# Cross-attention with a routed expert layer: the last 65 context rows laid out anew

## The reference

```
q = layernorm(x) @ Wq.T ; k = ctx @ Wk.T ; v = ctx @ Wv.T
attn = einsum('bhnc,bhlc->bhnl', q * 256 ** -0.5, k)
attn = softmax(attn, axis=2)
attn = attn / sum(attn, axis=-1, keepdims=True)
x = x + tanh(g_xattn) * (einsum('bhnl,bhlc->bhnc', attn, v) @ Wo.T)
x = x + tanh(g_ffn) * experts(layernorm(x))
```

## Time and profile before

| what | value |
|---|---|
| runs of the kernel before | 1812.7, 1813.04, 1815.76 us; median 1813.04 |
| profiled execution | 1814.16 us, span 1812.4 us |
| setup and first projections | to about 30 us of the span |
| attention, 8 batches | about 30 to 1245 us |
| turn to the experts, and the experts | 1245 us to the end |
| period of a middle batch | 152.6 us |
| mean granted clock | 0.991 |

### The profile page before, as it was taken

One profiled execution on the slowest core, in us unless ns is written; L12 is line 12 of the kernel. 1 busy time (PEld: TensorE's weight loads), 2 busy tenths in 40 slices (PEclk: granted clock), 3 DMA queues, 4 the chain that ended last, 5 costly groups with the idle time before them and its releaser, 6 DMA issues.

```text
span 1812.4 us, 31594 instructions
## 1 busy us (share of the span) xinstructions
PE 1683.1 (93%) x9980; PEld 900.1 (50%) x9980; DVE 1419.2 (78%) x2293; ACT 1283.9 (71%) x3640; POOL 542.7 (30%) x825
## 2 busy tenths in 40 slices
PE   8989999999999989999999998887799999999997
PEld 5223233333333323333333332214799999999997
DVE  7979999999999999999999999997444444444442
ACT  5989999999999999999999999995111111111111
POOL 3331251352244225235223422213222222222222
PEclk9999999999999999999999999999899999999999
DMA  8547215613711731461272163419222222222221
GB/s 233 129 112 189 63 51 148 162 40 96 196 53 52 176 108 47 133 181 40 75 194 60 58 162 83 148 54 299 86 35 38 36 37 35 38 35 38 35 36 28
DMA packets 128245, 172.87 MB, mean 95 GB/s; under 512 B 14496, under 2 KB 105760, under 8 KB 128128
## 3 DMA queue, kind: packets, MB, share of 16 engines
q1 hardware_dynamic: 113152, 150.51, 30.3%
q0 software_dynamic: 14144, 20.44, 6.5%
q10 hardware_dynamic: 832, 0.53, 0.1%
HBM read 117.96 MB, written 53.47 MB: 95 GB/s over the span
## 4 chain that ended last, share of the span: by engine, by line
PE 36%; ACT 29%; DVE 20%; issue 7%; POOL 3%; DMA 3%; SPq 1%; POOLq 0%; DVEq 0%; ACTq 0%
ACT w_all L899 27%; DVE negmax L1080 14%; PE scores L1474 13%; PE scores L1487 13%; PE scores L716 3%; PE acc L729 3%; POOL routed_rows L1273 1%; DVE resid L975 1%; ACT w_all L857 1%; DMA out<-row_t,gate_token 1%; PE spare L579 1%; PE spare L573 1%; PE spare L1464 1%; DVE rz L1066 1%; SPq L389 1%
## 5 line engine op out<-in xcount | busy, mean ns | idle before, releaser
L899 ACT ACTIVATE w_all<-scores,negmax 128x512 f32<-128x512 f32 (+1 forms) x1664 | 1127.8, 751 | 24.8 <-DVE negmax L1080 19.3
L1080 DVE TENSOR_REDUCE negmax<-scores 128x2 f32<-128x1024 f32 (+1 forms) x832 | 1002.2, 1216 | 65.6 <-PE scores L716 59.2
L716 PE MATMUL scores<-q_stack,w_all 128*128 128x512 bf16 (+1 forms) x1664 | 501.9, 383 | 50.0 <-ACT w_all L899 48.3
L899 ACT ACTIVATION_READ_ACCUMULATOR w_all<-scores,negmax 128x1 f32 (+1 forms) x1664 | 449.3, 270 | 0.0
L729 PE MATMUL acc<-w_all,vz 128*32 128x512 f32 (+1 forms) x3328 | 443.7, 605 | 3.0 <-POOL vz L1296 2.8
L1515 ACT ACTIVATE projections<-scores 128x512 f32<-128x512 f32 x142 | 84.9, 598 | 449.0 <-PE scores L1474 449.0
L716 PEld LDWEIGHTS scores<-q_stack,w_all 128*128 128x128 bf16 (+1 forms) x1664 | 115.7, 99 | 524.9 <-ACT w_all L899 395.5
L1296 POOL TENSOR_TENSOR vz<-w_all,rz 128x68 f32<-128x68 f32 (+1 forms) x416 | 124.7, 300 | 789.3 <-DVE rz L1066 763.7
L1474 PEld LDWEIGHTS scores<-row_t,q_stack 128*128 128x128 f32 x2272 | 265.9, 193 | 7.6 <-issue 2.8
L1474 PE MATMUL scores<-row_t,q_stack 128*128 128x128 f32 x2272 | 267.5, 276 | 2.0 <-DVE row_t L1542 1.8
L1487 PE MATMUL scores<-room,projections 128*128 128x256 f32 x1136 | 256.8, 379 | 0.0
(11 more groups left out here) (208 smaller groups left out, 1027.8 us busy)
## 6 DMA issues: line engine op xcount, KB each, us to landing
w_all<-k_parts SPq DMA_DIRECT2D x248, 200.1 KB, 3.5
w_all<-in_w SPq DMA_DIRECT2D x16, 1024.0 KB, 10.8
q_stack<-q_parts SPq DMA_DIRECT2D x248, 64.0 KB, 3.4
k_parts<-parts SPq DMA_DIRECT2D x42, 300.0 KB, 2.9
w_all<-in_ctx_t SPq DMA_DIRECT2D x7, 1601.0 KB, 7.3
parts<-routed SPq DMA_DIRECT2D x71, 129.0 KB, 2.1
q_parts<-parts SPq DMA_DIRECT2D x14, 384.0 KB, 3.2
routed<-pad_row SPq DMA_DIRECT2D x8, 645.0 KB, 9.5
```

What stands on the lines that cost most here:

```text
L716: mm = pe.matmul(scores[0:r, 2 * (u % SLOTS) + j % 2, :], k_stacks[g][:, j, lt * P:lt * P + r], q_stack[:, g, j, :], start=True, stop=True)
L899: e = act.activation(probs[0:r, s % RING, j, :], scores[0:r, 2 * (u % SLOTS) + j % 2, :], ACT.Exp, bias=negmax[0:r, u % 4, j % 2:j % 2 + 1 ...
L1080: dve.tensor_reduce(negmax[0:r, u % 4, :], scores[0:r, 2 * (u % SLOTS):2 * (u % SLOTS) + 2, :], AX.X, ALU.max, negate=True).then_inc(negma ...
```

## The change

The 65 rows of the last tile are split: 64 rows (`REST`) and the row 1600 (`LONE`).

- **Two heads in a tile.** The last step of a group (`lt == LT`, now 12) has one unit instead of two. Four matmuls of 64 columns of weights put heads 0 and 1 into one bank, one at partitions 0 to 63 and the other at 64 to 127, and heads 2 and 3 into the other bank. One reduction and two exponentials do for the four heads. The values of the tile stand twice, in both halves of the partitions, and are multiplied by 0 or 1 (`own_rows`) so that each head finds only its own half; `weigh` uses one bank of exponentials for two heads.
- **The lone row.** Row 1600 of all 16 heads stands in one tile. The context gets columns of zeros around row 1600 (`LK` = 1635 columns, `lone_apart` on the input), and matmuls of 32 columns of weights, shifted by the group, put head j of group g at partition 32 j + g and zeros elsewhere, adding up over the groups. In batches 1 to 7 this is one extra unit of 16 matmuls, one reduction of 512 and one exponential at the last step of group 0 (step 12); in batch 0 it is done for two groups at a time, after groups 0 and 2 (`lone_groups`). Its values (row 1600 on all partitions, masked by head) are scaled once by GpSimd (`lone_vz`), and every `weigh` of a last tile gets four more matmuls with them.
- **Units are counted through** over all batches (`units_by`), and each waits for `u - SLOTS + 1`. A batch has 101 units (102 in the first).
- **The last value piece** (tiles 12 and 13, the doubled 64 rows and the lone row) is done in two halves like the others, one step later in the table (48 for 47; in the first batch 7 for 6), and is taken by VectorE with the mask instead of by ScalarE; two fills behind it move on by one.
- VectorE writes the masks at the start with some 30 small memsets.

```diff
-LT = (L + P - 1) // P
+LT = L // P
+LAST_TILE = LT * P
+REST = L - 1 - LAST_TILE
+LONE = LAST_TILE + REST
+LONE_AT = LONE + H // 4 - 1
+LK = LONE_AT + TAIL_ROWS
+VT = LT + 2
+GROUP_STEPS = LT + 1
...
-    47: ("next", "v", 6), 48: ("cur", "attn_turn", 0), 49: ("cur", "o_turn", 2),
+    48: ("next", "v", 6), 49: ("cur", "attn_turn", 0), 50: ("cur", "o_turn", 2),
...
+def lone_groups(b, g):
+    if b == 0:
+        return range(g, g + 2) if g % 2 == 0 else range(0)
+    return range(G) if g == 0 else range(0)
+
+def units_of(b, s):
+    g, lt = s // GROUP_STEPS, s % GROUP_STEPS
+    return 2 if lt < LT or len(lone_groups(b, g)) else 1
...
         def project_v(bank, i, halves):
+            for lt in (2 * i + h for h in halves):
+                cols = slice((lt % 2) * D, (lt % 2 + 1) * D)
                 for k in range(KC):
+                    if lt == LT:
+                        for twice in range(2):
+                            mm = pe.matmul(bank[REST * twice:REST * (twice + 1), cols], ctx_sb[:, k, LAST_TILE:LAST_TILE + REST],
+                                           wv_sb[:, k, :], start=(k == 0), stop=(k == KC - 1))
+                    else:
+                        rows = ctx_sb[:, k, lt * P:(lt + 1) * P] if lt < LT else ctx_sb[:, k, LONE_AT:LONE_AT + 1].to_broadcast([P, P])
+                        mm = pe.matmul(bank[:, cols], rows, wv_sb[:, k, :], start=(k == 0), stop=(k == KC - 1))
...
         def unit_scores(b, s, p):
+            if p >= units_of(b, s):
+                return
...
-            wait(pe, exp_done, b * UNITS + (u - SLOTS + 1 if u >= SLOTS else (-1, 0, -2)[u]))
+            if lt == LT and p == 1:
+                for of in lone_groups(b, g):
+                    stack_here(b, of)
+            wait(pe, exp_done, u - SLOTS + 1)
...
+            elif p == 0:
+                for j in range(GH):
+                    mm = pe.matmul(scores[REST * (j % 2):REST * (j % 2 + 1), bank + j // 2, :],
+                                   k_stacks[g][:, j, LAST_TILE:LAST_TILE + REST], q_stack[:, g, j, :], start=True, stop=True)
+            else:
+                groups = lone_groups(b, g)
+                for of in groups:
+                    for j in range(GH):
+                        mm = pe.matmul(scores[32 * j:32 * j + TAIL_ROWS, bank, :],
+                                       k_stacks[of][:, j, LONE_AT - of:LONE_AT - of + TAIL_ROWS], q_stack[:, of, j, :],
+                                       start=(of == groups[0]), stop=(of == groups[-1]))
...
         def weigh(b, s):
...
+                mm = pe.matmul(acc[32 * j:32 * j + 32, :], vz[:, s % RING, j, :],
+                               probs[:, s % RING, j if lt < LT else j // 2, :], start=(lt == 0), stop=False)
+            if lt == LT:
+                pe.wait_ge(lone_vz_ready, lone_units(b, g))
+                for j in range(GH):
+                    mm = pe.matmul(acc[32 * j:32 * j + DH + 1, :], lone_vz[:, g * GH + j, :], lone_probs[:, :],
+                                   start=False, stop=True)
...
+            elif name in ("v", "own_v"):
+                dve.tensor_tensor(v_ones[(b + 1 if name == "v" else b) % 2][:, LT:VT, :, 0:DH],
+                                  spare[:, :].rearrange("p (t h c) -> p t h c", t=2, h=H),
+                                  own_rows[:, :, :].unsqueeze(3).to_broadcast([P, 2, H, DH]), ALU.mult).then_inc(fill_taken, 1)
...
+            if lt == LT and units_of(b, s) == 2:
+                groups = lone_groups(b, g)
+                heads = slice(groups[0] * GH, (groups[-1] + 1) * GH)
+                pool.wait_ge(lone_rz_ready, lone_units(b, g))
+                pool.tensor_tensor(lone_vz[:, heads, :], v_ones[b % 2][:, LT + 1, heads, :],
+                                   lone_rz[:, :].unsqueeze(2).to_broadcast([P, len(groups) * GH, DH + 1]),
+                                   ALU.mult).then_inc(lone_vz_ready, 1)
```

More of the change, by code:

```diff
@@ L138, in halves @@
         now, after = self.fill(s), self.fill(s + 1)
-        begun = after and after[0] in HALVED and after not in LAST_V
+        begun = after and after[0] in HALVED
         assert not (begun and now) or now[0] in HALVED
         if now:
-            split = now[0] in HALVED and now not in LAST_V
+            split = now[0] in HALVED
             return [(now, (1,) if split else (0, 1))]
@@ L883, in run @@
                             act.wait_ge(early_stored[at], 16)
-                if s < STEPS - 1 and it.fill(s) and it.fill(s)[0] != "logits":
+                if s < STEPS - 1 and it.fill(s) and it.fill(s)[0] != "logits" and it.fill(s) not in LAST_V:
                     take(it, *it.fill(s))
@@ L918, in _ @@
         dve.wait_ge(dve_setup, DVE_SETUP)
+        own = Chain(dve, own_rows_step, 0)
+        own(dve.memset(own_rows[:, :, :], 0.0))
+        own.settle()
+        own(dve.memset(own_rows[0:REST, 0, 0::2], 1.0))
+        own(dve.memset(own_rows[REST:P, 0, 1::2], 1.0))
+        for g in reversed(range(G)):
+            for j in range(GH):
+                own(dve.memset(own_rows[32 * j:32 * j + g + 1, 1, g * GH + j:g * GH + j + 1], 1.0))
+            own.settle()
+            if g:
+                for j in range(GH):
+                    own(dve.memset(own_rows[32 * j:32 * j + g, 1, g * GH + j:g * GH + j + 1], 0.0))
+        own.settle()
+        for tiles in v_ones:
+            own(dve.tensor_copy(tiles[:, LT:VT, :, DH], own_rows[:, :, :]))
+        own.settle()
         def bc(ap):
```

167 lines of the change are left out of this document (88 added, 79 removed).

## The result

The changed kernel takes 1822.57 us (median of 5 runs, 1820.26 to 1830.14) against 1813.04: a ratio of 1.0053, 95% interval 1.0043 to 1.0064. The forecast was 1788 us. The profiled execution took 1820.66 us with a span of 1818.9, 6.5 us more than the 1812.4 of before.

A forecast was written before the change was run, and what follows sets the result against it. Three engines stood within 5%, ScalarE fullest, TensorE to be fullest after. Six middle batches giving 19.2 us, the last 3.3 and the first 2.3 made 24.8 off 1814.16, 1789.4, less 1.1 for the median: 1788 us, range 1772 to 1805.

The forecast's parts named there:

- Above it I keep 0.6, 0.9, 0.5 and 0.7 us: Middle batch, four groups: time kept above each group's fullest engine for waits, giving 149.4 us against 152.62.
- rival 1: TensorE: narrow tiles don't overlap, a middle batch takes 2.0 us more, about 1823 us in all; chance 0.09.
- Prices of the new instructions: Middle batch: four 64-column scores 0.44 or 0.88 us, sixteen lone scores 0.9, lone values 1.00 a group, GpSimd scaling 0.6.
- TensorE becomes the fullest engine: Middle batch: TensorE's busy time rises by 4.0 to 146.4 us, ahead of ScalarE at 144.3 and VectorE at 141.6.
- over 10 us of idle: Sign in the profile after: TensorE idle that long in a batch, as before, would show the forecast wrong.
- ScalarE: 146.0, not 144.3: Middle batch: ScalarE falls from 149.24 to 144.3 us, 4.69 from seven exponentials and 0.25 from the last value copy.
- The one-unit steps: Ends of groups: seven exponentials go from a middle batch, at 0.67 us each, 4.69 us off ScalarE.
- rival 2: New waits (reciprocals, lone scaling, context load) eat most of the gain: 2.4 us more a batch, 1803 us; chance 0.15.
- The turn of the batch: Start of a batch: with units numbered through, the idle of 0.70 us on ScalarE and 1.13 on TensorE goes.
- Masks at nothing: Kernel start: VectorE builds masks before its 3.29 us wait for the first x; uncovered, some 2 us once.
- First batch: First batch: loses six exponentials but its context load comes later, a gain of 2.3 us.
- Last batch: Last batch: 4.7 us of seven exponentials less 1.0 for lone values and 0.4 for new waits, a gain of 3.3.

The follow-up runs named there:

- e5: The kernel before with one part of the change, units counted through over the batches: 1805.76 us, ratio 0.9945 to before.
- e3: The changed kernel without the lone value matmuls, so row 1600's share of the result is missing: 1801.69 us, ratio 0.9935 to the kernel before.
- e4: The kernel before with four zero-weight value matmuls added behind each group's last tile, ahead of the accumulator copy: 1833.57 us, ratio 1.0107 to before.
- e2: The changed kernel with the lone value matmuls moved from a group's last tile to its second, where ready: 1819.62 us, ratio 1.003 to the kernel before.
- e10: The changed kernel with masks by one copy, batch 0's last value projection unsplit, ready-made lone value matmuls directly before TensorE's waits: 1809.82 us, ratio 0.9963 to before.
- e9: The changed kernel with key part rows in DRAM 1664 columns apart, not 1635: 1823.89 us, ratio 1.0049 to the kernel before.

## Why the prediction was wrong

**The failed step** is "Above it I keep 0.6, 0.9, 0.5 and 0.7 us", with the sum of each engine's busy time as the bound under it. Above those bounds a batch kept 1.4, 2.2, 1.7 and 1.1, together 6.4 in place of 2.7. The bounds themselves, 146.7 together, weren't the failure: the fullest engine of each group has 37.4, 36.5, 37.0 and 35.9, together 146.8. Where I went wrong is the overlap. Of the 31 us between the forecast span and the measured one, six middle batches make 22, the first batch 7.5, the last 1.9, the start 0.7, and the expert part gave 0.9 back.

The runs split a middle batch, forecast -3.2 and measured +0.5, into three: counting the units through -1.4 (e5), the packing without the lone values -0.9 (e5 to e3), the lone values +2.7 (e3 to after). I had treated the 4.0 us of lone values as filling TensorE up, when what matters is who stands behind them. I priced the matmuls and left out the instruction that waits for them: VectorE's copy, which the earlier trace rows show with an idle time of 0.0, so with no measured room. e3 and e4 put work at that place at 2.7 and 2.5 us a batch. But the copy is half of the story: with the copy's wait gone in three groups (e2) the same work cost 2.4, and only in front of TensorE's own waits did it become cheap (e10: 0.1 and 0.3 us in groups 1 and 2, nothing in group 3). What I had wrong is that TensorE's idle time would take the work wherever it stood.

The 1823 us of rival 1 hit the time, and that is luck: its narrow tiles that don't overlap aren't there.

Of the terms:

- *Prices of the new instructions: right.* Four scores of 64 columns last as long as two of 128, and from start to start 0.55 (forecast 0.44, or 0.88 one after the other); sixteen lone ones 0.87 (forecast 0.9); lone values 0.97 a group (1.0), of which 0.85 are new, since the value tile ahead of them takes 0.88 in place of 1.00; GpSimd 0.64 (0.6); reduction of half width 0.69 (0.68).
- *"TensorE becomes the fullest engine": not seen.* The view has TensorE at 143.0 us in the batch (forecast 146.4), ScalarE at 146.0. But records of matmuls are missing in it (last section); by my estimate TensorE has about 145.4 (e3's 141.95, where none is missing, and 4 x 0.85), level with ScalarE. The sign "over 10 us of idle" came up (153.1 less 143.0), and some 2.4 us of it are those holes.
- *ScalarE: 146.0, not 144.3.* Seven exponentials are gone, but its busy time fell by 3.2 and not 4.9. An exponential's own read of the sum (0.19 to 0.25 us) lies under the next one only if a next one follows: an exponential and its read end 0.79 us after its start, and the next starts after 0.66, so each stop lays 0.13 bare. The timelines of the batch have 12 stops before and 23 after, which makes about 1.4 of the 1.7 us (estimate). The idle time rose too, so taking work away helped less than its length. I had taken the pitch of 0.67 as the saving wherever it stood.
- *The one-unit steps gave back under half.* e5 to e3 is the packing without the turn: the ends fall by 2.6 us instead of 4.7, the others rise by 1.2, the copy steps by 0.6. 0.9 us of 4.7 reach the period. Part of it is rival 2: the reciprocals do wait for ScalarE (below), 0.3 to 0.75 in three groups (forecast 0.4). A wait I hadn't seen is TensorE's: with one unit in step 51 the value tile two steps back comes a unit sooner, ahead of its scaling (1.31 us below). What each of these costs by itself no run shows.

The waits of after (total us, times, longest):

```profile
DVE o_acc L1157 <- PE acc L793: 19.0, 31, 0.7
...
PE acc L788 <- POOL vz L1382: 13.7, 20, 1.3
...
DVE rz L1151 <- ACT w_all L960: 12.3, 24, 1.2
...
ACT parts L912 <- DMA k_parts<-parts: 7.6, 1, 7.6
```

And the step before the turn in the timeline, reciprocals, scaling and the late value tile one behind the other, with what ScalarE paid:

```profile
802.75 0.17 DVE L1151 RECIPROCAL rz<-z 128x4 f32<-128x4 f32 x1
...
803.00 0.29 POOL L1382 TENSOR_TENSOR vz<-w_all,rz 128x68 f32<-128x68 f32 x1 [1.48 <-DVE rz L1151]
...
803.35 1.06 PE L788 MATMUL acc<-w_all,vz 128*32 128x512 f32 x8 [1.31 <-POOL vz L1382]
...
806.25 0.69 ACT L960 ACTIVATE w_all<-scores,negmax 128x512 f32<-128x512 f32 x1 [0.60 <-DVE negmax L1167]
```

- *The turn of the batch.* That it goes was right on TensorE: no wait of 1.13 is left. ScalarE's 0.70 became 0.60, since another wait took its place. Alone (e5) the turn is worth 1.4 us a batch, more than the packing's 0.9, and I had no term for it.
- *Masks at nothing: wrong.* Four memsets of one column take 0.40 us together, seven such groups follow each other every 0.45, and they end after the x has landed. VectorE's first statistics began at 5.88, now:

```profile
6.28 0.28 DVE L996 COPY w_all<-own_rows 128x32 f32<-128x32 f32 x2
6.59 0.75 DVE L1021 BATCH_NORM_STATS2 stats<-room 128x6 f32<-128x256 f32 x2
```

So +0.7 us, once. I had put them at 2 us; with the copies behind them they took 3.9, from 2.67 to 6.56.

- *First batch: forecast -2.3, measured +5.2*, the largest part of the loss. About 2.0 of it is the copy in three groups (steps 14, 27, 40). The context's load was issued 3.3 us later (52.09, before 48.76), as the value piece ahead of it ended a step later, and TensorE waited 1.17 us for it. The largest part, 2.9 us, is at step 23, where ScalarE waits for a store of key parts that stands on SP's queue behind sixteen stack loads. After (timeline, then two stretches in the view by stretch):

```profile
103.71 1.12 SPq L471 DMA_DIRECT2D k_parts<-parts  x2
...
111.14 0.52 ACT L912 ACTIVATE parts<-spare 128x409 bf16<-128x409 f32 x1 [7.61 <-DMA k_parts<-parts]
```

```profile
105.00:108.00 3.00, 0.00 (x0) 0.00 (x0) 0.00 (x0) 0.00 (x0) 0.11 (x1) 0.84 0.99 252
108.00:111.00 3.00, 0.00 (x0) 0.00 (x0) 0.00 (x0) 0.00 (x0) 0.00 (x0) 0.50 0.11 26
```

Before, the same place:

```profile
100.21 1.12 SPq L436 DMA_DIRECT2D k_parts<-parts  x2
105.01 0.50 ACT L848 ACTIVATE parts<-spare 128x400 bf16<-128x400 f32 x1 [4.68 <-DMA k_parts<-parts]
```

The DMA engines are busy 99% until 108, and then 11% for the last 3 us (the last two columns are the share and GB/s): the load is done but for a remainder that comes slowly, and the store is not counted as landed. Before, nothing trailed like that: 79% in the last 2 us before the landing (103 to 105). From the first load's issue to the landing it is 18.2 us against 15.3; the kernels with the old layout took 14.9 to 15.3, those with the new one 16.1 to 18.2. The bytes of a key load grew by 2%, against 5 to 22% in time; e9 didn't settle it. The waits of this batch also trade with each other: e3's store wait is 2 us shorter than after's, and its step 10, where TensorE waits for the context, 2.5 us longer. So no single one of them is the price of the new layout. I had priced the wider keys by their TensorE time only.

- *Last batch: forecast -3.3, measured -1.4.* It has the same copy waits, of 0.3 to 0.6 us, with ScalarE idle 3.6 us in place of 1.1.

Two rules beside these rows. In the timeline the 32-column values give way to the lone ones after 0.88 us, and to 128-column scores after 1.00; the lone ones give way to 128-column scores after 0.97. So a change of tile shape shows as about 0.1 us, near the 0.08 that I took. The Trainium skill, TensorEngine Tiling (Array Packing), Key Properties, has a drain at each change of mode; the trace agrees that a change has a price, about 0.1 us here, and doesn't show whether it is a drain. And VectorE's copy of the accumulator lasts 692 ns after the change and 680 before, while the packed scores took what was forecast; the same page of the Trainium skill, PSUM Bottleneck, says that tiling speeds up TensorE but not the emptying of PSUM, where the accumulator stands. The trace agrees.

## What to carry to other kernels

Price an added instruction by who waits for it and what is queued behind the waiter, and by whether its engine waits just there, not by its engine's free time over a whole stretch. A wait with an idle time of 0.0 in the trace has no known slack: bound it by the whole length of what is put in front of it. Where work must be added to a nearly full engine, put it directly in front of a wait of that engine that ends by itself: the same 3.9 us cost 2.7 behind the last tile, 2.4 with three of four groups moved to the second tile, and 0.9 with the three in front of waits. And when a change bundles several parts, price each alone: one part of this one, the counting of units, was worth by itself as much as the whole change at its best (e5 and e10: 151.2 us a batch both).

## What the runs showed of the hardware that was not expected

- TensorE's busy time in a view is only that of the matmuls that were recorded. Before and e5 issue the same matmuls, and a middle batch shows 142.40 us busy in the earlier trace rows and 140.28 in e5:

```profile
641.47:792.70 151.23, 140.28 (x785) 49.73 (x792) 144.82 (x235) 148.84 (x439) 54.38 (x94) 1.00 0.40 108
```

The page of e5 says why. Its weight loads are complete, and matmuls are missing, all of them among the scores of 128 columns:

```profile
L717 PE MATMUL scores<-q_stack,w_all 128*128 128x512 bf16 (+1 forms) x1551 | 476.9, 383 | 59.0 <-ACT w_all L900 43.1
...
L717 PEld LDWEIGHTS scores<-q_stack,w_all 128*128 128x128 bf16 (+1 forms) x1664 | 115.0, 99 | 517.0 <-ACT w_all L900 394.9
```

Before has 9980 matmuls to 9980 weight loads; the changed kernel has 10306 to 10428, and e3 10172 to 10172. Where the first of a pair is missing the timeline shows a lone "x1" with a hole of 0.16 us in front, as at 790.67 in e5. In the middle batch 16 of 192 are missing after and 15 in e5; before and e3 have all 192. At 0.16 us each that makes up to 2.6 and 2.4 us (estimate) on top of 143.0 and 140.3. That is why the lone values, 3.9 us from start to start, raised the busy time from e3 (141.95) to after (143.00) by only 1.05. Compare the counts of matmuls and weight loads before a bound of "the fullest engine" is read to a tenth.

- The mask memsets of one column on one to four rows, at rows 0, 32, 64 and 96, start 0.11 us apart, so 28 of them with their waits took 3.2 us (3.05 to 6.28). Those of one column on all 128 rows just ahead of them start some 0.02 us apart (2.12 to 2.47 for sixteen). Both are recorded with 59 ns; what makes the difference is open.
- The tail of a queue of loads: 3 us at 11% of the DMA engines' time before the store behind them counted as landed.
- The stall in the first batch goes on costing after it. TensorE does nothing from 105 to 112.4 us, and the granted clock is 0.50, the level of 1.2 GHz, from 108 to 117: the eight passes of a value tile last 1.94 us (below) in place of 1.06. Before, the shorter stall had a granted clock of 0.50 from 107 to 109. What this adds to the batch isn't separated by any run.

```profile
114.06 1.94 PE L788 MATMUL acc<-w_all,vz 128*32 128x512 f32 x8
```
